# Attention maxima on a split TensorE array: two heads per issue instead of one

## What is computed

```python
qkv = x @ Wqkv + bqkv
att = einsum('bhqd,bhkd->bhqk', q, k) * scale
att = softmax(where(causal, att, -inf))
x = layernorm(x + (att @ v) @ Wout + bout)
h = silu(x @ w1 * s1) * (x @ w2 * s2)      # weights are -1, 0, 1, times a scale
h = gelu(h @ h1 * sh1); h = gelu(h @ h2 * sh2)
x = layernorm(x + h @ w3 * s3)
```

## Time and profile before

| | |
|---|---|
| median of 3 runs | 2168.74 us (2168.48 to 2174.09) |
| span of the profiled execution | 2166.8 us |
| what lies around the span | 1.9 us against the median |
| TensorE busy | 2118.4 us, 98% |
| VectorE, ScalarE, GpSimd busy | 1259.9, 1316.1, 492.9 us |

### The profile page before, as it was taken

One profiled execution on the slowest core, in us unless ns is written; L12 is line 12 of the kernel. 1 busy time (PEld: TensorE's weight loads), 2 busy tenths in 40 slices (PEclk: granted clock), 3 DMA queues, 4 the chain that ended last, 5 costly groups with the idle time before them and its releaser, 6 DMA issues.

```text
span 2166.8 us, 52048 instructions
## 1 busy us (share of the span) xinstructions
PE 2118.4 (98%) x16294; PEld 1878.8 (87%) x16294; DVE 1259.9 (58%) x3928; ACT 1316.1 (61%) x2807; POOL 492.9 (23%) x899
## 2 busy tenths in 40 slices
PE   8789999999999999999999999999999999999998
PEld 4368889989889888899989889988999898988998
DVE  7765555556555565556556565565556556565452
ACT  6456566666556666566666666666566666656553
POOL 2222122221222222122221122222122132122220
PEclk9889999999999999999999999999999999999999
DMA  8742332232322332332232322333232232321100
GB/s 275 239 120 63 77 71 70 61 81 64 90 65 61 82 74 69 75 69 73 61 81 64 90 64 62 81 76 73 71 76 70 56 82 69 83 64 37 37 6 10
DMA packets 95940, 167.69 MB, mean 77 GB/s; under 512 B 19204, under 2 KB 38404, under 8 KB 95672
## 3 DMA queue, kind: packets, MB, share of 16 engines
q1 hardware_dynamic: 91912, 152.75, 28.6%
q10 hardware_dynamic: 3760, 11.54, 1.5%
HBM read 98.26 MB, written 68.17 MB: 77 GB/s over the span
## 4 chain that ended last, share of the span: by engine, by line
PE 89%; DVE 1%; DMA 0%; issue 0%; SPq 0%; ACT 0%; POOL 0%; POOLq 0%; DVEq 0%
PE ring L1241 44%; PE ring L1226 10%; PE pM L1116 7%; PE pS L1104 6%; PE pO L1164 6%; PE ring L1254 5%; PE ring L1176 4%; PE ring L1206 2%; PE ring L1196 2%; PE ring L1148 1%; PE ring L1215 1%; DMA qk_d<-c 0%; SPq L614 0%; DVE full_g L960 0%; DMA Qs<-nm 0%
## 5 line engine op out<-in xcount | busy, mean ns | idle before, releaser
L921 DVE CUSTOM_DVE_ANT_0 pM<-pM,mask 128x512 f32<-128x512 f32 (+3 forms) x1024 | 498.7, 502 | 366.1 <-PE pM L1116 292.3
L1241 PE MATMUL ring<-Yhi,H 128*128 128x256 f32 x1984 | 501.7, 289 | 0.0
L1241 PE MATMUL ring<-Xhi,H 128*128 128x256 f32 x1984 | 497.9, 288 | 0.0
L1241 PE MATMUL ring<-Ylo,H 128*128 128x256 f32 x1984 | 489.2, 282 | 0.0
L1241 PE MATMUL ring<-Xlo,H 128*128 128x256 f32 x1984 | 486.4, 282 | 0.0
L1241 PEld LDWEIGHTS ring<-Ylo,H 128*128 128x128 f32 x1984 | 377.8, 190 | 7.2 <-issue 3.4
L1241 PEld LDWEIGHTS ring<-Yhi,H 128*128 128x128 f32 x1984 | 377.0, 190 | 7.1 <-issue 3.4
L1241 PEld LDWEIGHTS ring<-Xlo,H 128*128 128x128 f32 x1984 | 379.1, 191 | 0.8
L1241 PEld LDWEIGHTS ring<-Xhi,H 128*128 128x128 f32 x1984 | 378.4, 191 | 1.0 <-issue 0.2
L1116 PE MATMUL pM<-Ks,Qs 128*128 128x512 f32 x992 | 304.2, 340 | 20.6 <-DVE mx L921 9.0
L865 ACT ACTIVATE Yhi<-ring,cols 128x256 fp32r<-128x256 f32 x248 | 117.8, 475 | 266.8 <-PE ring L1241 170.1
(11 more groups left out here) (146 smaller groups left out, 3518.7 us busy)
## 6 DMA issues: line engine op xcount, KB each, us to landing
qk_d<-c SPq DMA_DIRECT2D x120, 256.0 KB, 3.4
Qs<-qk_d SPq DMA_DIRECT2D x120, 192.0 KB
Ks<-qk_d SPq DMA_DIRECT2D x120, 192.0 KB
qk_d<-c SPq DMA_DIRECT2D x120, 128.0 KB, 3.0
xTs<-in_xT SPq DMA_DIRECT2D x16, 512.0 KB, 4.3
raw<-in_h SPq DMA_DIRECT2D x8, 1024.0 KB, 10.4
xz<-in_x SPq DMA_DIRECT2D x16, 512.0 KB, 3.9
H<-raw ACTq DMA_DIRECT2D x8, 1024.0 KB, 9.3
```

Source lines behind the costliest of these rows:

```text
L921: nc.vector.tensor_tensor_reduce(pM[:, h % 2, 0:n], pM[:, h % 2, 0:n], mask[:, T - n:T], 1.0, NEG, ALU.add, ALU.max, mx[:, t, h:h + 1]).th ...
L1241: mm = nc.tensor.matmul(to, w, x_part, start=(k == 0 and m == 0), stop=(k == KB - 1 and m == 1))
```

## The change

For blocks 2 and 3 (384 and 512 columns) a pair's two heads are scored by two matmuls of 64 rows each, one on the upper and one on the lower half of the rows of the array. The zero rows of the other head are no longer read. Both write all 128 partitions of their own bank of `pM`. Both wait until both banks are free (`need(pe, m_done, nth)` in place of `nth - 1`; the second has no wait of its own). For this the odd head's step is moved in the lists to right behind the even head's, by `heads_together`, for all engines. A block is taken this way only where all its four heads are in the iteration's list (`tiled`), and never in the opening list.

```diff
--- before.py
+++ after.py
@@ -57,6 +57,7 @@
 VW = D + 1
 EXP_UNITS = [0, 4, 8, 10, 11]
 MISC = 3
+TILED = 2
 
 
 ORDER = """
@@ -196,10 +197,26 @@
     return [(s[0], s[1], tuple(s[2:])) for s in steps]
 
 
-STEPS = plan(ORDER)
+def tiled(steps, off, g, t):
+
+    return t >= TILED and all(("max", off, (g, t, h)) in steps for h in range(G))
+
+
+def heads_together(steps):
+
+    out = list(steps)
+    for kind, off, a in steps:
+        if kind == "max" and a[2] % 2 == 0 and tiled(steps, off, *a[:2]):
+            odd = (kind, off, (*a[:2], a[2] + 1))
+            out.remove(odd)
+            out.insert(out.index((kind, off, a)) + 1, odd)
+    return out
+
+
+STEPS = heads_together(plan(ORDER))
 TURN = 1 + STEPS.index(("h_act", -2, ("h2", 1, 2)))
 HEAD = plan(HEAD_ORDER)
-FIRST = plan(FIRST_ORDER)
+FIRST = heads_together(plan(FIRST_ORDER))
 TAIL = plan(TAIL_ORDER)
 
 PARTED = {"h1": 2, "h2": 2, "ffn_out": 1, "y": 1}
@@ -1112,6 +1129,15 @@
                         nth = b * HEADS + (g * TB + TB - 1 - t) * G + h
                         if t == TB - 1 and h == 0:
                             pe.wait_ge(*stack_landed(steps, off, b, g))
+                        if steps is not HEAD and tiled(steps, off, g, t):
+                            if h % 2:
+                                continue
+                            need(pe, m_done, nth)
+                            for s in range(2):
+                                rows = slice(SROWS * s, SROWS * (s + 1))
+                                nc.tensor.matmul(pM[:, s, 0:n], Q[rows, h // 2, s, t * P:(t + 1) * P],
+                                                 K[rows, h // 2, 0:n], start=True, stop=True).then_inc(m_ready, 1)
+                            continue
                         need(pe, m_done, nth - 1)
                         nc.tensor.matmul(pM[:, h % 2, 0:n], Q[:, h // 2, h % 2, t * P:(t + 1) * P],
                                          K[:, h // 2, 0:n], start=True, stop=True).then_inc(m_ready, 1)
```

## The result

| | before | after |
|---|---|---|
| median of the runs, us | 2168.9 (2168.48 to 2174.09, 4 runs) | 2212.0 (2209.93 to 2216.14, 4 runs) |
| ratio | 1 | 1.0199, 95% interval 1.0185 to 1.0212 |
| span of the profiled execution, us | 2166.8 | 2214.4 |

The change costs 43 us, where 45 were forecast. The execution that was profiled is the longest of its four (2216.14 us), so the two spans differ by 4.5 us more than the medians do. I take sums from the medians and single prices from the trace, and set both side by side at the end.

The account below looks back on a forecast made before the run. TensorE's matmul slots were taken to bound the kernel. Saving 44.8 us against 89.7 us of switching, with moved work at nothing, put 44.9 us on the 2168.7 us median: 2213.6 us, range 2160 to 2258.

Parts of the forecast that it names:

- The bound: Whole kernel: the number and length of matmul slots on TensorE, busy 98% of the span, set the end.
- The saving: Maxima's pairs on TensorE: one slot of two removed, 0.22 us (512) and 0.17 us (384), 44.8 us in all.
- The switching: Into and out of the split array around each pair: 0.39 us a visit, 230 pairs, 89.7 us in all.
- rival 1: At the pairs: splitting only rows empties nothing, weights load ahead and halves run side by side; 2123.9 us, chance 0.17.
- No emptying: At the pairs: splitting only rows costs no switch, so the whole 44.8 us is saved; 2123.9 us, chance 0.17.
- half the price: At the pairs: only exposed loads or only emptying, 0.20 or 0.19 us a pair; 2166 to 2171 us, chance 0.12.
- Loads in series: At the pairs: the two weight loads run one behind the other, 21 us more; 2234 us, chance 0.17.
- No overlap: At the pairs: halves don't run together, switching paid and nothing saved, 44.8 us more; 2258 us, chance 0.09.
- What was moved: Odd heads issued beside even ones, also on VectorE, needing both pM banks: costed at nothing.
- the tight place: At 767.77, tightest of a batch's 16 pairs: VectorE done before the pair's turn; otherwise 0.5 us x 14 = 7 us.
- the up to 0.7 us later steps in the gate stage: VectorE's steps at L953 and L960, passed by odd maxima: taken as nothing, at worst 0.7 us a place.

Follow-up runs that it names:

- run 5: Changed kernel with four pairs of each steady iteration moved beside a weighted sum, three right ahead of one and one right behind: 2210.1 us, ratio 1.0190.
- run 8: Changed kernel's order, but every head scored over all 128 rows and waiting for its own bank alone, as before the change: 2171.8 us, ratio 1.0019.
- run 1: Changed kernel with both heads of a pair scored over all 128 rows again; the new order and wait for both banks stay: 2175.9 us, ratio 1.0036.
- run 7: Changed kernel with only the 512-column pairs on 64 rows, the 384-column pairs over all rows; order and waits kept: 2190.5 us, ratio 1.0102.
- run 2: Changed kernel with the order and waits of before; each head of the two wider blocks uses 64 rows, issued apart: 2283.8 us, ratio 1.0525.
- run 3: Changed kernel with each pair's two matmuls issued twice in a row, the second time over the first results: 2254.3 us, ratio 1.0399.
- run 6: Changed kernel with all four blocks of a group scored in pairs, also those of 256 and 128 columns: 2259.4 us, ratio 1.0418.
- run 4: Changed kernel with only the 512-column blocks in pairs; 384-column blocks have the order, waits and matmuls of before: 2202.6 us, ratio 1.0157.

## Why the prediction was right

**The bound** was right. TensorE sets the end before and after, and of the 48 us between the two profiled executions only 4 are time without a matmul.

**The saving: right.** The two halves run together. By the medians over all pairs in the trace of the changed kernel, the second half starts 3 ns behind the first (0.01 us taken), and the pair takes one slot.

**The switching: right in kind, a little too dear.** Over all pairs the medians are, from the start of the last full matmul of 256 columns to the pair 209 to 211 ns where it would be 120 (0.09 in, as forecast); from the first half to the next full matmul 431 ns (512) and 373 (384), that is, the exposed load of 0.10, the slot of 0.23 or 0.18, and some 0.09 of emptying; and 223 ns instead of 120 for that matmul (0.10). In all a pair of 512 takes 0.09 + 0.43 + 0.10 = 0.62 instead of 0.47, one of 384 takes 0.57 instead of 0.36. Before rounding that is 0.16 and 0.21 us more: 114 x 0.16 + 116 x 0.21 = 42 us. The forecast had 45. It also had each pair alone between full matmuls, and 15 of the pairs of 384 columns stand right ahead of the weighted sum, where one costs 0.19 less (run 5): 3 us, which leaves some 40. Two accounts of the whole, by the medians of the runs and by the profiled executions (there from the start of the first maximum to that of the last, which leaves the opening and the end out; before has 1994.35 us in it, the changed kernel 2039.74):

| step | by | medians, us | traces, us |
|---|---|---|---|
| the order | run 8 less before | 3.6 | 1.0 |
| the wait for both banks | run 1 less run 8 | 4.1 | 3.4 |
| 114 pairs of 512 columns split | run 7 less run 1 | 14.6 | 16.7 |
| 116 pairs of 384 columns split | the change less run 7 | 21.5 | 24.3 |
| sum | | 43.8 | 45.4 |

The splitting is 36 us by the one and 41 by the other. The two differ because the profiled execution of the changed kernel is 4.1 us above its median and that of run 1 is 2.1 below its own. Each ratio is known to 0.1 or 0.2%, 2 to 3 us, so they don't contradict each other; more than that the runs don't settle.

The rule of the Trainium skill, "TensorEngine Tiling (Array Packing)", Tiling Modes, Key Properties, that a change of mode drains the engine, holds for rows too: 0.09 us on the way in and about as much on the way out. The span of a packed group in the Trainium skill's page "TensorE: Matmul & The Clock Gate", Part 3 holds as well (3 ns for the second tile here), but only within a visit; it leaves out the 0.38 us of going there and back, and by itself would have given rival 1.

**The rivals.** No emptying (2124) and half the price (2166 to 2171) are excluded by the interval and by the 0.09 at both ends. Loads in series (2234) is excluded by the pair's loads, two in one record of 0.19 us. No overlap (2258) is excluded by run 2, where a head alone takes as long as a pair.

**What was moved: the term that failed.** I costed it at nothing, with 7 us as the worst at the tight place. Run 1 shows 7.7 us. It isn't at the tight place: VectorE was through there in time, as forecast, in run 1's trace at 767.64 us with the pair at 767.77. Nor is it the up to 0.7 us later steps in the gate stage, where the waits rose by 0.3 us in all. Runs 8 and 1 divide it into 3.6 us for the order and 4.1 for the wait for both banks; the traces have 1.0 and 3.4, and of the 3.4 one gap of Wout's matmuls in the last pass makes up 1.6. I had no term for any of it. Why the new order and the wait for both banks cost this stays open. That the forecast came within 2 us of the result is in part two errors that met: the switching 4 to 9 us too high, the moving 4 to 8 us too low.

## What to carry to other kernels

On this kernel a visit to a split array between full matmuls costs some 0.38 us, whatever is done in it, and a pair saves one slot (0.23 us at 512 columns). By this estimate two pairs of 512 columns in a visit would save 0.46 and begin to pay; no run here has such a kernel (run 3's second pair does no work of use). Right beside the weighted sum a visit costs 0.19 us, by the prices of run 5, and the pair should about pay for itself; that is an estimate too, and the run's time doesn't show such a gain. Before splitting, count the visits, not the matmuls, and see whether the buffers allow two groups in a row; here `pM` has two banks, which is one pair. If they don't, zero rows in a full matmul were the cheaper way here.

## What the runs showed of the hardware that I had not expected

- Splitting the rows and splitting the columns are different layouts to the array: a pair right ahead of the weighted sum takes 0.37 us to it, as to a full matmul, so the array empties between the two. It empties once, not twice, which makes the sum a cheaper neighbour than a full matmul (run 5).
- On a change of layout the weights aren't brought in ahead, and the price goes by their width, at the two widths that the traces have: the sum's first record behind a pair is 12 ns longer than its later ones with loads of 17 columns (604 and 592 ns), and the slot of a full matmul behind a pair is 103 ns longer with loads of 128.
- A maximum of 128 columns between full matmuls takes 0.115 us of TensorE, though the next matmul starts 0.06 us behind it: the time comes out one matmul later (run 6).
- TensorE's jump back at the end of a pass took 3.5 to 3.7 us in three of five passes of one kernel (run 4) and 0.36 to 0.48 in all the others. In the profiled execution that put 7.3 us of waiting into a loop whose source differs from the changed kernel's in one constant; the cause is open.
